# Expert feed-forward on TensorE: tokens transposed six parts ahead instead of four, and the low half of the tokens read last

## The chip, the cores and the metric

The kernel is one program on one NeuronCore of a Trainium2 chip. The metric is device time in microseconds; the times of repeated executions and one profiled execution are given. The engines are TensorE (PE in the profile, with its weight loads as PEld), VectorE (DVE), ScalarE (ACT), GpSimd (POOL) and SyncE (SP), which only issues transfers here.

## What is computed

A cross-attention layer and then a mixture-of-experts feed-forward, in float32. The change lies in the second. Cut to what matters:

```python
# 16 experts, each takes its 256 best tokens out of 4096; D = 256, F = 1024
_, idx = jax.lax.top_k(logits.T, 256)
xe = xn[idx]                                             # [16, 256, 256] gathered tokens
h = jnp.einsum('ecd,efd->ecf', xe, fc1_weight) + fc1_bias[:, None, :]
h = jax.nn.gelu(h, approximate=False)
y = jnp.einsum('ecf,edf->ecd', h, fc2_weight) + fc2_bias[:, None, :]
contrib = (y * gates[:, :, None]).reshape(-1, d)
output = jnp.zeros((n_tokens, d)).at[idx.reshape(-1)].add(contrib)
```

## The kernel before, in words

The attention part takes the first 790 us of the span and is not touched. A search for each expert's limit follows, and from 843 us on the experts run one after the other.

Precision is kept by splitting: a float32 operand is written as a high part (a rounded copy, made by ScalarE) and a low part (the rest, made by VectorE or GpSimd), and a product of two such operands is three fast products: high by high, low by high, high by low. `xe_hi` and `xe_lo` are the two parts of an expert's tokens, `w1_hi` and `w1_lo` those of its first weights. Some products take plain float32 operands; TensorE runs each of them as two instructions.

For one expert `e` the pieces of work are:

- `gather`: GpSimd issues two indirect transfers that bring the 256 token rows into `gathered`.
- `turn_tokens`: TensorE transposes them, four 128x128 blocks into one PSUM bank (line 1175). ScalarE scales the bank into `xe_hi` (two instructions), and then VectorE makes `xe_lo` from the bank and `xe_hi` (line 2107, two instructions). The signal `xe_hi_made` (semaphore tokens_high) tells of the first, `xe_emptied` (semaphore tokens_split) of the second.
- `hidden(e, f)`, f = 0 to 7: the first product of the expert for 128 of the 1024 hidden values, six matmuls of 256 columns into one of four banks. ScalarE applies the gelu (`h_full`), and for f = 0 to 3 of the experts from 2 on the result is split as well (`h_hi`, `h_lo`).
- `expert_out(e, c, f)`: one of the eight parts of the second product, for token half c. For f = 0 to 3 it is three fast matmuls (`in_parts`), for f = 4 to 7 one float32 matmul (two instructions). Half c = 0 takes f in the order 0 to 7, half c = 1 in the order 4, 5, 6, 7, 0, 1, 2, 3. Experts 0 and 1 use float32 for all parts.
- `gate`, `scale_out`, `scatter`: bias, gate value, and the transfer that adds the rows to the output.
- `split`, `split_out`: the weights of the next experts are split (ScalarE, then GpSimd or VectorE). `list_hot`, `list_count`, `list_join`, `list_spread`: which tokens belong to a later pair of experts.

One list, `schedule_experts()`, sets the order of all of it. Each engine's program walks the list and takes the kinds that concern it. Within an expert a counter `at` goes up after every `hidden` and every `expert_out`, 24 in all, and `between()` adds the other work at given counts. Waits are issued through `Waits.wait_ge`, which skips a wait for a value that the engine has already waited for, so that a wait in `hidden` for the tokens is issued once per expert, at f = 0. In the rows of instructions below `w_0` with `h_full` is a float32 part of the second product, `w_hi` and `w_lo` are split weights: with `xe_hi`, `xe_lo` those of the first product, with `h_hi`, `h_lo` those of the second.

Of the kernel before, what the change touches and what calls it, by code (L numbers as in the profile page):

```python
# [26 lines left out]
E, F = 16, 1024  # L27
# [7 lines left out]
FT = F // P  # L35
# [310 lines left out]
def group_of(e):  # L346

    return e if e < 2 else e // 2 + 1


def schedule_experts():
    plan = []

    def add(*piece):
        plan.append(piece)
# [54 lines left out]
    def second_list(at):  # L410

        if at == 5:
            add("list_count", 2)
            add("list_join", 2)
        elif at == 7:
            add("list_spread", 2)
            add("gather", 2)
            add("gather_gates", 1)
# [7 lines left out]
    for e in range(1, E):  # L426
        lists = group_of(e + 3) if e % 2 and e + 3 < E else None
        counts = group_of(e + 2) if e % 2 == 0 and e + 2 < E else None
        state = {"point": 0}
        hot_points = (8, 9) if e == 1 else (9, 17)  # L430

        def between():

            state["point"] += 1
            at = state["point"]
            if e == 1:
                second_list(at)
            if at == 10 and e == 1:
                for c in range(2):
                    add("scale_out", 0, c)  # L440
            if at == 2 and counts:
                add("list_count", counts)
            if at == 5 and counts:
                add("list_join", counts)
            if at == 7 and counts:
                add("list_spread", counts)
            if at == (11 if e == 1 else 4):
                for c in range(2):
                    add("scatter", e - 1, c)
            if at == 9 and 2 < e + 1 < E:  # L450
                add("split", e + 1, 1)
            if at == 13 and e + 2 < E:
                add("split", e + 2, 0)
            if at == (12 if e == 1 else 10) and e + 2 < E:
                add("gather", e + 2)
            if at in hot_points and lists:
                add("list_hot", lists, hot_points.index(at))
            if at == 3 * FT - 4 and e + 1 < E:
                add("turn_tokens", e + 1)
            if at == 3 * FT - 2 and e + 1 >= SPLIT_FROM and e + 1 < E:  # L460
                add("split_out", e + 1)

        for f in range(FT):
            add("hidden", e, f)
            between()
        for c in range(2):
            for f in OUT_ORDER[c]:
                add("expert_out", e, c, f)
                between()
            add("gate", e, c)  # L470
            if e == E - 1:
                add("scale_out", e, c)
                add("scatter", e, c)
        if e < E - 1:
            for c in range(2):
                add("scale_out", e, c)
# [8 lines left out]
def _build(nc, io, everything):  # L485
# [3 lines left out]
    def signal(name):  # L489
        return Signal(semaphore(name))  # L490

    def sb(name, shape, dt, where=None):
        return (where or everything).enter_context(nc.sbuf_tensor(name, shape, dt))
# [85 lines left out]
    w1_hi, w1_lo = ([sb(f"w1_{n}{i}", [P, 2, F], F32R) for i in range(2)] for n in ("hi", "lo"))  # L579
# [5 lines left out]
    xe_hi, xe_lo = ([sb(f"xe_{n}{i}", [P, 2, CAP], F32R) for i in range(2)] for n in ("hi", "lo"))  # L585
# [61 lines left out]
    def token_key(e, c):  # L647

        return (e, c if c is not None else 1) if e == 0 else (e,)
# [55 lines left out]
    xe_hi_made = signal("tokens_high")  # L705
# [129 lines left out]
    turned, xe_emptied = signal("tokens_turned"), signal("tokens_split")  # L835
# [77 lines left out]
    def tensor_program(pe):  # L913
        on = Waits(pe)

        def mm(out, lhsT, rhs, start, stop):
            return pe.matmul(out, lhsT, rhs, start=start, stop=stop, skip_group_check=True)  # L917
# [260 lines left out]

        def hidden(e, f):
            i = e % 2  # L1180
            on.wait_ge(*xe_emptied.at(*token_key(e, 1)))
            for n in range(2):
                on.wait_ge(*w_lo_made.at(e, n))
            n = e * FT + f
            if n >= 4:
                on.wait_ge(*h_made.at(*hidden_order[n - 4]))
            to, cols, n = hidden_bank[n % 4][:, 0:CAP], slice(f * P, (f + 1) * P), 0
            for half in range(2):
                for w, x in ((w1_hi, xe_hi), (w1_lo, xe_hi), (w1_hi, xe_lo)):
                    last = mm(to, w[i][:, half, cols], x[i][:, half, :], n == 0, n == 5)  # L1190
                    n += 1
            last.then_inc(hidden_filled.sem, 1)

        def expert_out(e, c, f):
# [18 lines left out]
            if f == last_f:  # L1213
                last.then_inc(y_filled.sem, 1)

        work = {"search": search, "limits": limits, "rank": rank, "list_count": list_count, "list_spread": list_spread,
                "turn_tokens": turn_tokens, "hidden": hidden, "expert_out": expert_out}
        for kind, *at in expert_plan:
            if kind in work:
# [1119 lines left out]
```

## Time and profile before

| | us |
|---|---|
| median of 3 executions | 1089.4 (1089.0 to 1089.87) |
| profiled execution, its own time | 1088.49 |
| profiled execution, span of the core | 1086.7 |
| TensorE matmuls busy | 981.4 (90% of the span) |
| VectorE busy | 788.4 (73%) |
| ScalarE busy | 675.7 (62%) |
| GpSimd busy | 767.8 (71%) |

The span is the stretch from the first to the last instruction that the profiler recorded; the execution's own time lies 1.79 us above it. Busy times are sums over instructions and say nothing yet on which engine sets the end in a given stage.

### The profile page before, as it was taken

The page shows a single profiled execution, that of the slowest core. Times are in us where ns is not written, and L with a number is a line of the kernel's source. Part 1 is how long each engine was busy: PE and PEld are TensorE (multiplying, and loading weights), DVE is VectorE, ACT ScalarE, POOL GpSimd, SP SyncE. Part 2 cuts the span into 40 slices and gives each one's busy share as a digit, 9 for nine tenths or more (in the row PEclk, how much of TensorE's full clock was granted, in tenths as well). Part 3 has the DMA queues.
Part 4 walks back from the last instruction along what each step waited for, and adds up shares of the span by engine and source line. Part 5 has one row for each costly group of instructions (what it writes and reads, how often), then busy time and mean ns, then how long its engine had stood idle before and what let it go on. Part 6 is the DMA issues. An engine that isn't in the chain of part 4 may idle for free. (4 is left out here: it accounts for less than half of the span.)

```text
span 1086.7 us, 17837 instructions
## 1 busy us (share of the span) xinstructions
PE 981.4 (90%) x6102; PEld 651.6 (60%) x6102; DVE 788.4 (73%) x1925; ACT 675.7 (62%) x1352; POOL 767.8 (71%) x872
## 2 busy tenths in 40 slices
PE   4999999999999999999998999999811999999995
PEld 3665456555655655655564565444411889999995
DVE  6989778867977886887797677767588756666642
ACT  6775775766777677576757665554354446666662
POOL 4037997798698699679967967899313377777772
PEclk9899999999999999999999999999955899999998
DMA  7020020002012001210110001000174366666651
GB/s 188 1 63 2 6 59 1 1 28 59 1 27 80 1 1 54 54 50 12 46 46 2 4 1 42 13 1 21 40 194 129 41 182 197 197 205 205 205 167 20
DMA packets 73611, 71.82 MB, mean 66 GB/s; under 512 B 38928, under 2 KB 67568, under 8 KB 69424
## 3 DMA queue, kind: packets, MB, share of 16 engines
q1 hardware_dynamic: 66464, 61.92, 18.5%
q0 software_dynamic: 6272, 8.69, 4.6%
q8 instruction: 49, 0.80, 0.3%
q14 instruction: 42, 0.34, 0.1%
q10 hardware_dynamic: 784, 0.07, 0.1%
HBM read 56.83 MB, written 13.83 MB: 65 GB/s over the span
## 5 line engine op out<-in xcount | busy, mean ns | idle before, releaser
L1504 POOL TENSOR_TENSOR prob_sum<-prob_sum,probs 128x256 f32<-128x256 f32 x628 | 467.2, 775 | 79.4 <-ACT probs L1227 71.0
L917 PE MATMUL bank<-probs,v_nat 128*64 128x512 f32 x768 | 190.0, 609 | 0.5 <-ACT probs L1227 0.5
L1819 DVE CUSTOM_DVE_ANT_0 masked_scores<-score_pair,mask_bias 128x512 bf16<-128x512 f32 x142 | 92.1, 686 | 49.1 <-PE score_pair L917 47.8
L1227 ACT ACTIVATE probs<-score_pair,mask_col 128x512 f32<-128x512 f32 x128 | 81.0, 686 | 66.9 <-PE score_pair L917 64.6
L1227 ACT ACTIVATE probs<-pair_bank,mask_col 128x512 f32<-128x512 f32 x128 | 81.3, 690 | 49.5 <-PE pair_bank L917 37.1
L917 PEld LDWEIGHTS bank<-probs,v_nat 128*64 128x64 f32 x768 | 46.0, 136 | 84.2 <-issue 77.6
L1819 DVE CUSTOM_DVE_ANT_0 masked_scores<-pair_bank,mask_bias 128x512 bf16<-128x512 f32 x114 | 73.9, 685 | 25.4 <-PE pair_bank L917 24.0
L1570 POOL DMA_INDIRECT out_x<-y_out,token_index x32 | 54.9, 1714 | 40.6 <-DVE y_out L2139 36.0
L1534 POOL TENSOR_TENSOR w_lo<-w_raw,w_hi 128x1024 fp32r<-128x1024 f32 x28 | 66.4, 2371 | 20.9 <-ACT w_hi L1227 20.5
L1504 POOL TENSOR_TENSOR prob_sum<-probs 128x256 f32<-128x256 f32 x64 | 44.9, 733 | 46.7 <-ACT probs L1227 40.0
L1812 DVE TENSOR_REDUCE maxima<-pair_bank 128x2 f32<-128x1024 f32 x42 | 51.1, 1217 | 25.2 <-PE pair_bank L917 24.9
L1227 ACT ACTIVATE h_full<-bank,b_cols 128x256 f32<-128x256 f32 x96 | 44.1, 468 | 35.8 <-PE bank L917 35.7
L1482 POOL TENSOR_TENSOR z_lo<-z_full,z_hi 128x512 fp32r<-128x512 f32 x32 | 40.9, 1280 | 33.9 <-ACT z_hi L1227 33.9
L917 PE MATMUL bank<-xe_hi,w_hi 128*128 128x256 f32 x192 | 57.7, 300 | 5.9 <-DVE xe_lo L2107 5.9
L1850 DVE RECIPROCAL bank<-bank 128x128 f32<-128x128 f32 x64 | 57.3, 934 | 3.4 <-PE bank L917 3.4
L917 PE MATMUL bank<-w_ctx_hi,z_hi 128*128 128x512 f32 x128 | 56.9, 445 | 0.8 <-POOL z_hi L1482 0.8
L917 PE MATMUL bank<-xe_hi,w_lo 128*128 128x256 f32 x192 | 54.5, 284 | 0.0
L917 PE MATMUL bank<-xe_lo,w_hi 128*128 128x256 f32 x192 | 54.5, 284 | 0.0
L1227 ACT ACTIVATE squares<-bank 128x256 f32<-128x256 f32 (+1 forms) x96 | 44.2, 460 | 15.8 <-PE bank L917 8.5
L1617 DVE TENSOR_REDUCE sq_sum<-squares 128x4 f32<-128x256 f32 (+1 forms) x96 | 46.0, 497 | 9.2 <-ACT squares L1227 9.1
L1227 ACT ACTIVATE probs<-pair_bank 128x512 f32<-128x512 f32 x58 | 31.4, 594 | 32.4 <-PE pair_bank L917 27.9
L1227 ACT ACTIVATE probs<-score_pair 128x512 f32<-128x512 f32 x70 | 38.0, 596 | 21.4 <-PE score_pair L917 19.1
(278 smaller groups left out, 2796.6 us busy)
## 6 DMA issues: line engine op xcount, KB each, us to landing
w_raw<-in_fc SPq DMA_DIRECT2D x16, 1024.0 KB, 4.9
w<-in_fc SPq DMA_DIRECT2D x16, 1024.0 KB, 5.8
c_in<-in_ctx SPq DMA_DIRECT2D x16, 384.0 KB, 4.1
x_in<-in_x SPq DMA_DIRECT2D x8, 512.0 KB, 5.0
out_x<-x_in SPq DMA_DIRECT2D x8, 512.0 KB, 3.9
rows_scratch<-xr_nat SPq DMA_DIRECT2D x8, 512.0 KB, 3.0
c_in<-in_ctx SPq DMA_DIRECT2D x16, 128.0 KB, 4.2
b_rows<-in_fc_bias SPq DMA_DIRECT2D x16, 128.0 KB, 5.6
```

The lines of the kernel that those rows point to most:

```text
L917: return pe.matmul(out, lhsT, rhs, start=start, stop=stop, skip_group_check=True)
L1227: return act.activation(out, a, f, bias=bias, scale=scale)
L1482: tt(to[place][rows, half, :], z_full[rows, half, :], as32(z_hi[place][rows, half, :]), ALU.subtract).then_inc(z_lo_made.sem, 1)
L1504: last = tt(total[:, half], first[:, half], p[:, half], ALU.add)
L1534: tt(w1_lo[i][:, n, :], w1_raw[i][:, n, :], as32(w1_hi[i][:, n, :]), ALU.subtract).then_inc(w_lo_made.sem, 1)
L1570: pool.indirect_dma_start(out_rows, bass.IndirectOffsetOnAxis(ap=tokens_of(e, c), axis=0), y_out[i][:, c, :], None, compute_op=ALU.add).th ...
L1617: dve.tensor_reduce(sq_sum[:, place:place + heads], squares[square_turn[use] % 2][:, 0:heads * DH].rearrange("p (h d) -> p h d", d=DH), AX ...
L1812: last = dve.tensor_reduce(maxima[:, :, j, g], place[:], AX, ALU.max)
L1819: last = dve.tensor_tensor_reduce(masked_scores[:, hh, :], place[:, hh, :], mask_bias[:, 512 * g:512 * (g + 1)], 1.0, MASKED, ALU.add, ALU ...
L1850: state["inverse", pair, quarter] = step.of(dve.reciprocal(sums, sums))
```

## The change

The transposes of the next expert's tokens are placed in the list when 18 of an expert's 24 pieces are issued, in place of 20, except in expert 1, where they stay at 20. And `hidden` waits at its head for the high part of the tokens alone, issues the four matmuls that read it, waits for the low part, and issues the two that read that. The number of instructions stays the same on every engine.

```diff
@@ schedule_experts()
                 add("gather", e + 2)
             if at in hot_points and lists:
                 add("list_hot", lists, hot_points.index(at))
-            if at == 3 * FT - 4 and e + 1 < E:
+            if at == (3 * FT - 4 if e == 1 else 3 * FT - 6) and e + 1 < E:
                 add("turn_tokens", e + 1)
@@ tensor_program: hidden(e, f)
             i = e % 2
-            on.wait_ge(*xe_emptied.at(*token_key(e, 1)))
+            on.wait_ge(*xe_hi_made.at(*token_key(e, 1)))
             for n in range(2):
                 on.wait_ge(*w_lo_made.at(e, n))
@@
             for half in range(2):
-                for w, x in ((w1_hi, xe_hi), (w1_lo, xe_hi), (w1_hi, xe_lo)):
-                    last = mm(to, w[i][:, half, cols], x[i][:, half, :], n == 0, n == 5)
+                for w in (w1_hi, w1_lo):
+                    mm(to, w[i][:, half, cols], xe_hi[i][:, half, :], n == 0, False)
                     n += 1
+            on.wait_ge(*xe_emptied.at(*token_key(e, 1)))
+            for half in range(2):
+                last = mm(to, w1_hi[i][:, half, cols], xe_lo[i][:, half, :], False, half == 1)
             last.then_inc(hidden_filled.sem, 1)
```

Two places of TensorE's row of instructions show what moved. The first is the second token half of expert 5, where the tokens of expert 6 are transposed (`ident,gathered`). Before:

```order
L917 MATMUL bank<-w_0,h_full 128x256 [waits hidden_made] x4
L917 MATMUL pair_bank<-w_0,h_full 128x256 [waits y_emptied]
L917 MATMUL pair_bank<-w_0,h_full 128x256 x3
L1175 MATMUL score_pair<-ident,gathered 128x128 [waits gathered2]
L1175 MATMUL score_pair<-ident,gathered 128x128 x3
L917 MATMUL pair_bank<-w_hi,h_hi 128x256
```

In the changed kernel, at the same place:

```order
L917 MATMUL bank<-w_0,h_full 128x256 [waits hidden_made] x4
L917 MATMUL pair_bank<-w_0,h_full 128x256 [waits y_emptied]
L917 MATMUL pair_bank<-w_0,h_full 128x256
L1175 MATMUL score_pair<-ident,gathered 128x128 [waits gathered2]
L1175 MATMUL score_pair<-ident,gathered 128x128 x3
L917 MATMUL pair_bank<-w_0,h_full 128x256 x2
L917 MATMUL pair_bank<-w_hi,h_hi 128x256
```

The four transposes went ahead of two float32 matmuls (four instructions on the chip, since each is run as two). No other row lies between.

The second place is the hand-over to the next expert, the end of expert 5's second product and expert 6's first `hidden`. Before:

```order
L917 MATMUL pair_bank<-w_hi,h_lo 128x256
L917 MATMUL bank<-xe_hi,w_hi 128x256 [waits expert_w_low,tokens_split]
L917 MATMUL bank<-xe_hi,w_lo 128x256
L917 MATMUL bank<-xe_lo,w_hi 128x256
L917 MATMUL bank<-xe_hi,w_hi 128x256
L917 MATMUL bank<-xe_hi,w_lo 128x256
L917 MATMUL bank<-xe_lo,w_hi 128x256
```

In the changed kernel:

```order
L917 MATMUL pair_bank<-w_hi,h_lo 128x256
L917 MATMUL bank<-xe_hi,w_hi 128x256 [waits expert_w_low,tokens_high]
L917 MATMUL bank<-xe_hi,w_lo 128x256
L917 MATMUL bank<-xe_hi,w_hi 128x256
L917 MATMUL bank<-xe_hi,w_lo 128x256
L917 MATMUL bank<-xe_lo,w_hi 128x256 [waits tokens_split]
L917 MATMUL bank<-xe_lo,w_hi 128x256
```

The two matmuls that read `xe_lo` went to the end of the group, and the wait for tokens_split went with them. On VectorE, ScalarE, GpSimd and SyncE no row moved.

## Rows read from the trace of the kernel before

**Rows 1.** Head of the page.

```profile
span 1086.7 us, 17837 instructions
```

**Rows 2.** Windows: two experts, the first products of expert 0, a stretch near 880.

```profile
core 0: us, PE busy (x) PEld busy (x) DVE busy (x) ACT busy (x) POOL busy (x), PEclk, DMA share, GB/s
925.07:953.09 28.02, 27.20 (x219) 25.48 (x219) 17.33 (x30) 17.41 (x34) 20.50 (x13) 1.00 0.65 197
...
847.35:851.30 3.95, 3.95 (x16) 3.38 (x17) 1.87 (x3) 1.55 (x3) 1.39 (x1) 0.50 0.26 71
...
878.60:882.00 3.40, 3.40 (x11) 2.80 (x10) 1.77 (x3) 1.78 (x3) 2.79 (x3) 0.50 0.54 56
```

**Rows 3.** Waits of the weight loads, 880 us to the end: total, times, longest.

```profile
PEld bank L917 <- DVE xe_lo L2107: 8.0, 13, 0.6
```

**Rows 4.** Timeline of TensorE, hand-over from expert 5 to 6: start, duration, instruction.

```profile
934.02 1.89 PE L917 MATMUL pair_bank<-w,h_full 128*128 128x256 f32 x8
935.75 0.60 PE L1175 MATMUL score_pair<-ident,gathered 128*128 128x128 f32 x4
936.11 0.36 PE L917 MATMUL pair_bank<-w_hi,h_hi 128*128 128x256 f32 x1
...
937.38 0.28 PE L917 MATMUL pair_bank<-w_lo,h_hi 128*128 128x256 f32 x1
937.50 0.28 PE L917 MATMUL pair_bank<-w_hi,h_lo 128*128 128x256 f32 x1
938.19 0.38 PE L917 MATMUL bank<-xe_hi,w_hi 128*128 128x256 f32 x1 [0.41 <-DVE xe_lo L2107]
938.41 0.28 PE L917 MATMUL bank<-xe_hi,w_lo 128*128 128x256 f32 x1
```

**Rows 5.** Timeline of GpSimd, VectorE and ScalarE over the same hand-over.

```profile
932.58 2.35 POOL L1534 TENSOR_TENSOR w_lo<-w_raw,w_hi 128x1024 fp32r<-128x1024 f32 x1
...
935.14 1.21 DVE L2068 TENSOR_TENSOR hot_ids<-hot_lo,tile_ids 128x1024 bf16<-128x1024 bf16 x1
...
936.39 0.84 ACT L1227 ACTIVATE xe_hi<-score_pair,nw_col 128x256 fp32r<-128x256 f32 x2 [2.96 <-PE score_pair L1175]
...
937.12 1.06 ACT L1227 ACTIVATE w_hi<-w 128x1024 fp32r<-128x1024 f32 x1
...
937.26 0.87 DVE L2107 SCALAR_TENSOR_TENSOR xe_lo<-score_pair,nw_col,xe_hi 128x256 fp32r<-128x256 f32 x2 [0.91 <-ACT xe_hi L1227]
```

**Rows 6.** A gather for expert 7, its landing times, and the transposes that read it.

```profile
936.42 0.98 POOL L1552 DMA_INDIRECT gathered<-rows_scratch,token_index  x1 [0.30 <-issue]
...
DMA to landing us min/median/max: 2.8/5.0/6.3
...
950.64 0.60 PE L1175 MATMUL score_pair<-ident,gathered 128*128 128x128 f32 x4
```

**Rows 7.** Timeline of all engines, start of expert 0.

```profile
846.02 0.63 ACT L1227 ACTIVATE xe_hi<-score_pair,nw_col 128x128 fp32r<-128x128 f32 x2 [1.49 <-PE score_pair L1175]
...
846.15 0.58 PE L917 MATMUL bank<-earlier,all_ones 128*128 128x448 bf16 x1
...
846.68 0.61 DVE L2107 SCALAR_TENSOR_TENSOR xe_lo<-score_pair,nw_col,xe_hi 128x128 fp32r<-128x128 f32 x2
...
847.35 0.58 PE L917 MATMUL bank<-xe_hi,w_hi 128*128 128x256 f32 x1 [0.62 <-DVE xe_lo L2107]
847.73 0.41 PE L917 MATMUL bank<-xe_hi,w_lo 128*128 128x256 f32 x1
```

**Rows 8.** Chain that ended last, 847 to 879 us: start, duration, what.

```profile
855.69 0.88 DVE xe_lo L2107 x2
...
873.12 5.16 DMA gathered<-rows_scratch,token_index
```

**Rows 9.** Timeline of TensorE, end of expert 1.

```profile
878.33 0.92 PE L1175 MATMUL score_pair<-ident,gathered 128*128 128x128 f32 x4 [2.22 <-DMA gathered<-rows_scratch,token_index]
879.04 3.35 PE L917 MATMUL pair_bank<-w,h_full 128*128 128x256 f32 x8
```

## The prediction, made before the changed kernel was run

> **What bounds the kernel now.** The page gives the span, 1086.7 us [rows 1], and TensorE as the busiest engine. Busy shares don't say which wait costs time, so I read the expert stage by windows next. Over two consecutive experts, 28.02 us, TensorE's matmuls are busy 27.20 us at the full granted clock of 1.00, GpSimd 20.50, ScalarE 17.41 and VectorE 17.33 [rows 2]. TensorE sets the pace there, and only what makes it stop can be won. The waits from 880 us on name one stop alone that recurs: 13 times the weight loads stood still until VectorE's `xe_lo` was there, 8.0 us in all [rows 3]. These are the 13 hand-overs from one expert to the next, from expert 2 to 3 up to 14 to 15.
>
> The timeline shows one of them [rows 4]. The last matmul of expert 5 starts at 937.50, and the first of expert 6 at 938.19. The cause is a chain that begins with the transposes at 935.75. ScalarE starts `xe_hi` at 936.39, VectorE starts `xe_lo` at 937.26 and needs 0.87 [rows 5], and TensorE starts at 938.19, 0.06 after the end of `xe_lo`. From the transposes to the first product is thus 2.44 us, while the second product behind the transposes gives TensorE only 1.87 us of work (935.75 to 937.62).
>
> **What one stop costs.** The matmul row shows 0.41 idle, but matmuls are pipelined and overlap, so I take starts. Undisturbed fast matmuls start 0.12 apart (937.38, 937.50). From 937.50 to the second matmul of the next expert, at 938.41, pass 0.91, where two steps of 0.12 would do: 0.67 is lost [rows 4]. Times 13 that is 8.7 us. Taken from the weight loads it would be 8.0 [rows 3], and from the matmuls' idle time 13 x 0.41 = 5.3; these are the low bounds. The Trainium skill, page "Perfetto Trace Analysis", section "Identifying the Most-Contended Engine", says that matmul busy time is a poor measure of how near TensorE is to its limit, since pipelined instructions look smaller than they are, and that weight-load busy time is better. By that the sum would be 8.0 and not 5.3. The trace agrees in direction; the starts give a little more than either.
>
> **First edit: transposes two parts ahead.** They now pass two float32 parts, four of the eight instructions that start between 934.02 and 935.75, so 4 x 0.216 = 0.87 us [rows 4]. The whole chain moves up by that, if its engines are free. ScalarE is: it had been idle 2.96 us when `xe_hi` came [rows 5]. VectorE in this expert has a list to build, `hot_ids` until 936.35; `xe_lo` would be released at 937.26 - 0.87 = 936.39, so it just fits; the even experts make no such list. `xe_lo` is then ready for TensorE at 938.19 - 0.87 = 937.32, and TensorE comes for it at 937.62 at the earliest. The stop is gone, with 0.30 to spare.
>
> The transposes cost TensorE the same wherever they stand. The four take 0.36 from first start to the next instruction [rows 4]. What the trace doesn't show at full clock is transposes followed by float32 matmuls. At half clock it does: the first float32 matmul comes 0.71 behind four transposes [rows 9], no more than twice 0.36. The bounds are 0 and, from the step that is 0.10 longer after the present stop (938.19 to 938.41 against 0.12), 0.10 for each of 13, 1.3 us together. I take 0, since the row with the same sequence shows none.
>
> **Second edit: low part last.** The first four matmuls now need `xe_hi` only, which VectorE started to use at 937.26, and the low part is wanted four steps of 0.12 later, 0.48 us. Alone this edit would leave 938.19 - (937.62 + 0.48) = 0.09 of the stop. With the first edit in place it adds nothing in these 13 hand-overs but slack: 0.30 becomes 0.78. The added wait stands in front of two matmuls with nothing but later matmuls of TensorE behind it; it is issued once per expert and is satisfied when it comes. I take nothing for it: the list has such waits at most of the `hidden` pieces already, and TensorE's 27.20 busy plus two stops of 0.41 are the whole 28.02 of two experts [rows 2, 4], so a satisfied wait leaves no idle time.
>
> The second edit acts alone in expert 0. There TensorE stands from the end of a list product until `xe_lo` is there at 847.35, while `xe_hi` is done at 846.65 [rows 7]. The list product's row ends at 846.73, with a tail that overlaps the next matmul, and 0.06 behind `xe_hi` is 846.71: TensorE can start the first product there, 0.64 earlier. Sixteen matmuls take 3.95 at this clock [rows 2], about 0.25 each, so the four high ones reach past 847.35 and no second stop follows. What of the 0.64 reaches the end? The chain that ended last goes on through expert 0's first products, expert 1's `xe_lo` at 855.69, VectorE's gate work and list, the gather that lands at 878.3, and the transposes at 878.33 [rows 8, 9]. All of it hangs on TensorE here, so it moves along. But TensorE works at half clock until 851.3 (0.50) [rows 2]: if the clock rises at the same moment whatever TensorE does, 0.64 us gained at half speed is worth 0.32 afterwards. Bounds 0.3 and 0.64; I take 0.45, the middle.
>
> In expert 1 the transposes stay where they are, and behind them lie eight float32 instructions, enough. Nothing changes.
>
> **What comes next to the bound.** With the stop gone two experts take 28.02 - 1.34 = 26.68 us. GpSimd's 20.50 fits. Its `w_lo` for the next expert was done at 934.93 for a product at 938.19 [rows 5], 3.3 us early, and remains 2.6 early. VectorE's later work gets easier: the split of the second weights starts when ScalarE's `w_hi` ends, 938.18 before, and both move up with the transposes. The gather for expert 7 was issued at 936.42 and takes 5.0, at most 6.3, so it is there by 942.7, against 950.64 - 0.87 = 949.77 for its transposes, 7 us of slack [rows 6].
>
> **The sum.** 8.7 + 0.45 = 9.15 us off the profiled execution's own 1088.49 gives 1079.3. That execution lay 0.9 below the median of the three runs, so for the median 1089.4 - 9.15 = 1080.2.
>
> **The rivals.**
>
> *As forecast*, the 13 stops vanish and nothing takes their place: 1080.2. Chance 0.74.
>
> *A new wait takes part of it.* VectorE is the candidate in the experts that build lists, five of the 13: `hot_ids` ends only 0.04 before `xe_lo` would be released. For it speaks that margin; against it the 0.78 of slack behind. It would need to be 0.78 late there. If half of all the stops came back, the gain would be 4.35 + 0.45 = 4.8: 1084.6. Chance 0.10.
>
> *The clock falls out otherwise.* After TensorE's wait of 2.22 us for the gather, the granted clock is 0.50 from 878.6 to 882.0 [rows 2], and the four transposes and eight matmuls take 0.71 and 3.35 against 0.36 and 1.89 at full clock: 1.8 lost [rows 4, 9]. The first product starts earlier now, and everything behind lies differently against the clock. If this stretch is spared, 1078.4; if it comes twice, 1082.0. The three runs of before lie within 0.9 us, which speaks for a steady clock. Chance 0.10. The Trainium skill, page "TensorE: Matmul & The Clock Gate", section "What's actually happening", says that the moment of the clock's change isn't tied to the kernel's start and varies from run to run. By that rule both outcomes should turn up among single runs of either kernel; so far no run here shows it.
>
> *It doesn't bind.* If another engine or a transfer set the pace of two experts at 28.02, the stops would only change their name: 1089.4. Against it, no other engine exceeds 20.50 and no other wait recurs. Chance 0.03.
>
> *Slower.* The transposes now ask for the gathered rows 0.87 earlier and hold everything behind them on TensorE, since they stand in its queue. Were the rows late, the stop would lie there, in the middle of the second product. It decides when a landing takes over 13.3 us (936.42 to 949.77) instead of 5.0, and costs net from 14.0 on, 0.67 being won back. With rows 1 us late at all 13 it is 13 x 0.33 - 0.45 = 3.8 slower: 1093.2. In the trace only expert 2's rows came late [rows 9], and there the place is unchanged. Chance 0.03.
>
> **How the numbers follow.** A measurement of this kernel can tell about 0.2%, 2.2 us. Faster by more: forecast, part and clock, 0.94. Within: 0.03. Slower: 0.03. The likeliest case alone reaches from 1079.2 (8.7, 0.64, and 0.9 for the spread of the runs) to 1082.4 (weight-load count 8.0, 0.3, and the full 1.3 for the changed sequence). The range takes in the clock case on both sides and a small part of the second rival: 1078.3 to 1083.0, some 85 in 100.
>
> **What would show it.** In the profile of the changed kernel: the waits of the weight loads for `xe_lo` in the expert stage go from 13 times to none; the last matmul of an expert and the first of the next start 0.12 apart, at every hand-over; two experts take 26.7 us; `xe_lo` ends 0.3 us before the old first product's place; expert 0's first product starts right behind `xe_hi`, at about 846.7. The prediction is wrong if a wait of similar size appears under another name (gathered, `h_lo`, `w_lo`), if transposes between float32 matmuls cost a step, or if the granted clock of the stage differs from 1.00.

## The result, and the profile after

| | before | the changed kernel |
|---|---|---|
| median, us | 1089.2 (1086.79 to 1090.39, 6 runs) | 1079.34 (1077.77 to 1080.65, 6 runs) |
| profiled execution, its own time | 1088.49 | 1077.77 |
| span of the core | 1086.7 | 1075.9 |

The ratio of changed to before is 0.9916, 95% interval 0.9906 to 0.9926. That is a gain of 0.84%; by the ratio it is 9.15 us, by the two medians 9.9. The changed kernel was timed once more beside its variants (the last experiments below) and came out at 0.9919, interval 0.9907 to 0.9932.

The spans differ by 10.8 us, and 1.73 of that has nothing to do with the change: in this execution the part ahead of the experts ended earlier. The cut is the list product in front of expert 0's first product (`bank<-earlier,all_ones`), which starts at 846.15 before [rows 7] and at 844.42 after. What lies behind it differs by 9.07 us, against the 9.15 of the prediction's sum. That the two agree to 0.1 is partly luck: a second profiled execution of the changed kernel (`after_again` below) differs by 9.7 behind the same cut, since its clock fell out otherwise.

First the head of the changed kernel's page, then its windows over the two experts that correspond to [rows 2], from the first product of expert 5 to that of expert 7, and over a stretch near 880 us.

```profile
span 1075.9 us, 17837 instructions
```

```profile
core 0: us, PE busy (x) PEld busy (x) DVE busy (x) ACT busy (x) POOL busy (x), PEclk, DMA share, GB/s
921.02:947.75 26.73, 26.73 (x221) 25.39 (x220) 19.69 (x31) 17.39 (x34) 20.50 (x13) 1.00 0.68 209
877.30:880.70 3.40, 3.40 (x13) 2.87 (x12) 2.83 (x6) 1.41 (x3) 3.06 (x2) 0.50 0.68 77
```

Two experts take 26.73 us in place of 28.02, and the matmuls are busy in all of them. VectorE went from 17.33 to 19.69 us, although it executes the same instructions. The stretch at a granted clock of 0.50 (1.2 GHz of the two levels 1.2 and 2.4) is there as before, 3.4 us long.

The waits of the changed kernel's weight loads from 880 us on. The row of [rows 3] is gone, and what is left are five short waits of another kind:

```profile
PEld score_pair L917 <- DVE list_parts L2085: 0.8, 5, 0.2
```

The timeline of TensorE in the changed kernel, at the hand-over from expert 5 to 6, to be laid beside [rows 4]:

```profile
930.74 0.60 PE L1175 MATMUL score_pair<-ident,gathered 128*128 128x128 f32 x4
931.18 1.03 PE L917 MATMUL pair_bank<-w,h_full 128*128 128x256 f32 x4
...
933.35 0.28 PE L917 MATMUL pair_bank<-w_hi,h_lo 128*128 128x256 f32 x1
933.47 0.28 PE L917 MATMUL bank<-xe_hi,w_hi 128*128 128x256 f32 x1
...
933.95 0.40 PE L917 MATMUL bank<-xe_lo,w_hi 128*128 128x256 f32 x2
934.19 0.28 PE L917 MATMUL bank<-xe_hi,w_hi 128*128 128x256 f32 x1
```

The last product of expert 5 and the first of expert 6 start 0.12 apart, and it is 0.12 at the other twelve hand-overs too. From the transposes to the first product 2.73 us pass now, all of them work; before it was 2.44 with a stop in them.

GpSimd, VectorE and ScalarE over the same hand-over, for [rows 5]:

```profile
928.54 2.93 POOL L1537 TENSOR_TENSOR w_lo<-w_raw,w_hi 128x1024 fp32r<-128x1024 f32 x1
...
933.95 2.39 POOL L1537 TENSOR_TENSOR w_lo<-w_raw,w_hi 128x1024 fp32r<-128x1024 f32 x1
```

```profile
930.48 1.29 DVE L2070 TENSOR_SCALAR hot_ids<-hot_lo,token_in_tile 128x1024 bf16<-128x1024 bf16 x1
931.69 1.21 DVE L2071 TENSOR_TENSOR hot_ids<-hot_lo,tile_ids 128x1024 bf16<-128x1024 bf16 x1
932.82 0.86 DVE L2110 SCALAR_TENSOR_TENSOR xe_lo<-score_pair,nw_col,xe_hi 128x256 fp32r<-128x256 f32 x2
933.61 3.82 DVE L2118 TENSOR_TENSOR w_lo<-w,w_hi 128x1024 fp32r<-128x1024 f32 x1
```

```profile
931.38 0.84 ACT L1230 ACTIVATE xe_hi<-score_pair,nw_col 128x256 fp32r<-128x256 f32 x2 [2.10 <-PE score_pair L1175]
```

`xe_hi` is done at 932.22, but `xe_lo` doesn't start before 932.82, since VectorE still works at the list. It ends at 933.68, which is 0.21 us behind the start of the first product (933.47) and 0.27 ahead of the first product that reads it (933.95). In this expert it is the second edit that keeps TensorE from stopping.

Last, the start of expert 0 and the transposes of expert 2 in the changed kernel, for [rows 7] and [rows 9]:

```profile
844.42 0.58 PE L917 MATMUL bank<-earlier,all_ones 128*128 128x448 bf16 x1
...
844.97 0.29 PEld L917 LDWEIGHTS bank<-xe_hi,w_hi 128*128 128x128 f32 x1 [0.77 <-ACT xe_hi L1230]
844.97 0.58 PE L917 MATMUL bank<-xe_hi,w_hi 128*128 128x256 f32 x1
```

```profile
876.23 0.66 PE L1175 MATMUL score_pair<-ident,gathered 128*128 128x128 f32 x4 [1.96 <-DMA gathered<-rows_scratch,token_index]
876.73 3.09 PE L917 MATMUL pair_bank<-w,h_full 128*128 128x256 f32 x8
879.25 0.78 PE L917 MATMUL bank<-xe_hi,w_hi 128*128 128x256 f32 x1
```

The first product of expert 0 starts 0.55 behind the start of the list product, where it was 1.20. The wait for the gathered rows of expert 2 is 1.96 in place of 2.22.

To see what each stretch gave, the table sets out intervals between starts on TensorE's timeline for every kernel of this study, in us. A is the list product, 0, 2 and 3 are the first products of those experts, T the transposes of expert 2, and "end" is the last product of expert 15. The variants are told below.

| kernel | A to 0 | A to T | T to 2 | 2 to 3 | 3 to end | span |
|---|---|---|---|---|---|---|
| before | 1.20 | 32.18 | 3.72 | 14.98 | 178.40 | 1086.7 |
| the changed kernel | 0.55 | 31.81 | 3.02 | 15.06 | 170.37 | 1075.9 |
| after_again | 0.55 | 31.67 | 2.03 | 15.05 | 170.85 | 1075.9 |
| turn_only | 1.20 | 32.26 | 3.69 | 14.43 | 172.07 | 1079.5 |
| low_last_only | 0.55 | 32.14 | 3.48 | 14.67 | 172.82 | 1081.0 |
| expert0_only | 0.55 | 31.95 | 3.42 | 15.29 | 178.30 | 1086.4 |
| list_behind | 1.19 | 32.14 | 3.71 | 14.43 | 190.07 | 1099.0 |
| turn_16 | 1.19 | 32.31 | 3.71 | 14.40 | 188.81 | 1096.0 |
| half_pool | 0.55 | 30.03 | 2.03 | 14.41 | 170.23 | 1075.9 |
| e1_22 | 0.55 | 31.97 | 1.59 | 15.50 | 170.81 | 1076.1 |
| e1_24 | 0.55 | 31.87 | 1.59 | 15.16 | 170.35 | 1074.9 |
| gates_clear | 0.55 | 29.12 | 2.03 | 20.78 | 170.35 | 1080.0 |
| best | 0.55 | 29.75 | 1.53 | 20.03 | 170.38 | 1080.1 |
| early_list | 0.55 | 29.18 | 2.03 | 17.14 | 170.71 | 1076.2 |

Of the 9.07 us, 8.03 lie in the last stretch, with 12 of the 13 hand-overs: 0.67 each. The thirteenth, from expert 2 to 3, is hidden in the table: the half-clock stretch began 1.07 us behind the transposes of expert 2 instead of 0.27 (877.3 and 876.23, against 878.6 and 878.33), so that less of it lay ahead of expert 2's first product (3.72 became 3.02) and more behind (14.98 became 15.06). The two columns together, T to 3, went from 18.70 to 18.08: 0.62. From A to T 0.37 came from expert 0, and 0.05 lies behind the last product.

### The profile page after: what moved, and what is told of

It is laid out like the page before. It is cut to its first block and busy times, and to the rows that moved or that the text cites. A ratio compares the mean times of both kernels' runs of the same rounds, so it can differ in the third digit from the quotient of the medians.

```text
span 1075.9 us, 17837 instructions
## 1 busy us (share of the span) xinstructions
PE 975.3 (91%) x6102; PEld 649.4 (60%) x6102; DVE 801.7 (75%) x1925; ACT 675.0 (63%) x1352; POOL 768.3 (71%) x872
## 5 line engine op out<-in xcount | busy, mean ns | idle before, releaser
L1537 POOL TENSOR_TENSOR w_lo<-w_raw,w_hi 128x1024 fp32r<-128x1024 f32 x28 | 70.3, 2511 | 13.3 <-ACT w_hi L1230 13.1
L917 PE MATMUL bank<-xe_hi,w_hi 128*128 128x256 f32 x192 | 53.0, 297 | 0.0
L917 PE MATMUL bank<-xe_hi,w_lo 128*128 128x256 f32 x192 | 51.1, 287 | 0.0
L917 PE MATMUL bank<-w_ctx_lo,z_hi 128*128 128x512 f32 x128 | 51.0, 398 | 0.0
```

The lines of the kernel that those rows point to most:

```text
L1537: tt(w1_lo[i][:, n, :], w1_raw[i][:, n, :], as32(w1_hi[i][:, n, :]), ALU.subtract).then_inc(w_lo_made.sem, 1)
```

## The experiments

### Each edit alone

`turn_only` is the kernel before with the first edit, `low_last_only` with the second as its diff above shows it, and `expert0_only` with the second in expert 0 alone.

```diff
@@ turn_only: schedule_experts()
-            if at == 3 * FT - 4 and e + 1 < E:
+            if at == (3 * FT - 4 if e == 1 else 3 * FT - 6) and e + 1 < E:
@@ expert0_only: hidden(e, f)
-            on.wait_ge(*xe_emptied.at(*token_key(e, 1)))
+            on.wait_ge(*(xe_emptied if e else xe_hi_made).at(*token_key(e, 1)))
...
+            if e == 0:
+                passes = [(half, *p) for part in (high, low) for half in range(2) for p in part]
```

> The transposes stand six parts ahead, the first product reads its inputs in the old order with the one wait at its head. Theory of the prediction: the low part is there 0.30 us before it is wanted at all 13 hand-overs, so every stop vanishes, 8.7 us gained, ratio about 0.992, and the second edit is worth only the 0.45 us of expert 0. Rival, from the trace of the changed kernel: in experts 3, 5, 7, 9 and 11 VectorE is held up by its list work and the low part ends 0.22 us behind the first product's place; then five stops of about 0.38 us stay and the gain is 8.7 - 1.9 = 6.8 us, ratio about 0.994.

> The transposes stay four parts ahead, the first product reads the low part last. Theory of the prediction: 0.09 us of each stop stays at the low products, up to 0.2 with the slower restart behind a stop; gain 13 x 0.48 to 13 x 0.58 plus 0.45 in expert 0, 6.7 to 8.0 us, ratio 0.9927 to 0.9939. Rival that a wait in the middle of a group of products costs more than it hides: stops of 0.3 us and more stay, gain under 5 us.

> Only expert 0 reads the low part last; all else is as before. Theory: its first product starts 0.65 us earlier, and 0.3 to 0.64 us of that is left where expert 2's tokens are transposed, so that the stretch from the list product before expert 0 to those transposes is 0.3 to 0.64 us shorter than the 32.18 us of before. Rival: the gather's landing or VectorE's list sets that place whatever TensorE does, and the stretch stays at 32.2. In whole time both are within what a measurement can tell. The 13 stops of 0.67 us stay.

| | median, us | ratio to before, 95% interval |
|---|---|---|
| turn_only | 1081.8 | 0.9947 (0.9934 to 0.996) |
| low_last_only | 1081.87 | 0.9941 (0.9928 to 0.9954) |
| expert0_only | 1087.68 | 0.9991 (0.9979 to 1.0003) |

**Transposes ahead alone** leave the stop in five of the thirteen hand-overs. Waits of its weight loads from 880 us on:

```profile
PEld bank L917 <- DVE xe_lo L2107: 1.6, 5, 0.3
```

TensorE and VectorE at one of the five, expert 5 to 6:

```profile
935.65 0.28 PE L917 MATMUL pair_bank<-w_hi,h_lo 128*128 128x256 f32 x1
936.05 0.39 PE L917 MATMUL bank<-xe_hi,w_hi 128*128 128x256 f32 x1
936.28 0.28 PE L917 MATMUL bank<-xe_hi,w_lo 128*128 128x256 f32 x1
```

```profile
935.13 0.86 DVE L2107 SCALAR_TENSOR_TENSOR xe_lo<-score_pair,nw_col,xe_hi 128x256 fp32r<-128x256 f32 x2
```

The step is 0.40 where 0.12 is undisturbed. The other four, at 908.6, 962.7, 989.8 and 1016.8, look the same (0.38 or 0.40); all five follow an expert that builds a list (3, 5, 7, 9, 11). So the rival of the expectation is what came. The prediction's step that the first edit removes all thirteen stops by itself is wrong in these five. The last column of the table prices them: 172.07 against 170.37 with both edits, 1.70 us, 0.34 each.

**Low part last alone** takes 178.40 down to 172.82, 0.465 for each of twelve hand-overs, and leaves 0.205 of 0.67. The prediction left 0.09. Its gain, 6.4 us by the ratio, is just under the 6.7 that was the least expected. The timeline of TensorE in this kernel, same hand-over, shows the difference:

```profile
936.53 0.28 PE L917 MATMUL pair_bank<-w_hi,h_lo 128*128 128x256 f32 x1
936.65 0.28 PE L917 MATMUL bank<-xe_hi,w_hi 128*128 128x256 f32 x1
...
937.01 0.28 PE L917 MATMUL bank<-xe_hi,w_lo 128*128 128x256 f32 x1
937.22 0.50 PE L917 MATMUL bank<-xe_lo,w_hi 128*128 128x256 f32 x2
937.56 0.28 PE L917 MATMUL bank<-xe_hi,w_hi 128*128 128x256 f32 x1
```

The low products start 0.21 behind the fourth high one, 0.09 more than a step, as reckoned. But the two of them then take 0.34 to the next product, where two take 0.24 undisturbed (933.95 to 934.19 in the changed kernel). Behind the stop of [rows 4] the next step was 0.10 longer than the usual 0.12, and so it is here, where the stop is 0.09; 0.09 + 0.10 is the 0.2 that stayed. What makes that step longer no run shows.

**Expert 0 alone** moves its first product up by 0.65, and the transposes of expert 2 by 0.23 (32.18 to 31.95). Its total can't be told from that of the kernel before.

### Why VectorE is late in the list-building experts

In `list_behind` (the first edit, and the second list piece at 19 in place of 17) VectorE makes `xe_lo` before that piece; in `turn_16` the transposes stand at 16, without the second edit. Both clear `xe_lo`'s way.

```diff
@@ list_behind, beside the first edit
-        hot_points = (8, 9) if e == 1 else (9, 17)
+        hot_points = (8, 9) if e == 1 else (9, 19)
@@ turn_16
-            if at == 3 * FT - 4 and e + 1 < E:
+            if at == (3 * FT - 4 if e == 1 else 3 * FT - 8) and e + 1 < E:
```

> As turn_only, with the second piece of VectorE's list work for a later pair of experts placed behind the split of the tokens instead of ahead of it. If the list work ahead of it is what makes the low part late in five experts, all 13 stops vanish without the second edit: gain 8.7 us, ratio about 0.992, 1.9 us faster than turn_only. If VectorE is late for another reason (GpSimd's work on the weights at the same time), the five stops stay and the time is that of turn_only.

> First product in the old order, transposes eight parts ahead in place of six (expert 1 as before), so that VectorE's split of the tokens stands ahead of the second piece of its list work. Theory: what made the low part late in five experts with six parts ahead is that VectorE was still at that list piece; here the low part is ready about 0.9 us before it is wanted at all 13 hand-overs, no stop is left without the second edit, and the list piece is done before the long split of the second weights: 8.7 us gained, ratio about 0.992. Rival: the list piece is pushed back as it was with the list behind the split, the count of the list waits 2.8 us in five experts, and the time is above the kernel before.

Both are slower than the kernel before: 1099.79 us, ratio 1.0101 (1.0088 to 1.0114), and 1097.4, ratio 1.0091 (1.0077 to 1.0104). No stop for `xe_lo` is left at any hand-over, in either. That was expected, but a gain of 8.7 us with it; only the rival of `turn_16` forecast the loss. In the stops' place stands this, in `list_behind`, five times; TensorE, VectorE and GpSimd behind the hand-over to expert 6, and the window that follows:

```profile
941.98 0.28 PE L917 MATMUL bank<-xe_lo,w_hi 128*128 128x256 f32 x1
944.75 0.96 PE L917 MATMUL score_pair<-hot_ids,hot_hi 128*32 128x64 bf16 x15 [2.49 <-DVE hot_ids L2068]
```

```profile
940.64 3.97 DVE L2068 TENSOR_TENSOR hot_ids<-hot_lo,tile_ids 128x1024 bf16<-128x1024 bf16 x1
```

```profile
941.15 2.37 POOL L1534 TENSOR_TENSOR w_lo<-w_raw,w_hi 128x1024 fp32r<-128x1024 f32 x1
```

```profile
944.50:947.90 3.40, 3.15 (x38) 3.09 (x39) 2.77 (x7) 0.00 (x0) 1.28 (x1) 0.50 0.62 246
```

`hot_ids` takes 1.21 us elsewhere and 3.97 here, where GpSimd's subtraction for `w_lo` lies inside it. TensorE stops for 2.77 from start to start, and the granted clock is then 0.50 for 3.4 us. Against the changed kernel the last stretch of the table is 19.7 us longer (190.07 against 170.37), 3.94 for each of the five: 2.65 is the stop (2.77 less a step of 0.12), and the 1.3 that is left goes to the half clock. In `turn_16` it is the other `hot_ids` instruction, at 937.92: 3.38 us long, 0.49 elsewhere, with `w_lo` on GpSimd from 938.61 to 941.01. The stops are 2.43 there and the five together 18.4 us.

`half_pool` is the test of the cause: the changed kernel, with GpSimd's subtraction done for one half of the weights' columns only, for the experts from 2 on (the other half is left out, so the result isn't the reference's).

```diff
-                tt(w1_lo[i][:, n, :], w1_raw[i][:, n, :], as32(w1_hi[i][:, n, :]),
+                half = slice(0, F // 2)
+                tt(w1_lo[i][:, n, half], w1_raw[i][:, n, half], as32(w1_hi[i][:, n, half]),
```

> The changed kernel, with GpSimd's subtraction for the first weights cut to half of its columns from expert 2 on: half of w1_lo is then that of an earlier expert, which leaves part of the work out. If GpSimd and VectorE take turns at these subtractions, VectorE's split of the second weights (3.57 and 3.82 us beside GpSimd's 2.4) falls by about half of GpSimd's time, to 2.4 to 2.7, and the low part of the tokens in experts 3, 5, 7, 9 and 11 ends before the first product starts instead of 0.22 us behind. If VectorE is slow for its own reasons, both stay. The time stays within 1 us of the changed kernel, as TensorE has no stop there.

Groups of VectorE's instructions by line and form (count, busy us in all, mean ns of one, idle before), in the kernel before:

```profile
L2115 DVE TENSOR_TENSOR w_lo<-w,w_hi 128x1024 fp32r<-128x1024 f32 x14 | 34.8, 2484 | 1.0
L2067 DVE TENSOR_SCALAR hot_ids<-hot_lo,token_in_tile 128x1024 bf16<-128x1024 bf16 x7 | 4.0, 573 | 0.1
```

The same two in the changed kernel:

```profile
L2118 DVE TENSOR_TENSOR w_lo<-w,w_hi 128x1024 fp32r<-128x1024 f32 x14 | 47.0, 3355 | 0.6
L2070 DVE TENSOR_SCALAR hot_ids<-hot_lo,token_in_tile 128x1024 bf16<-128x1024 bf16 x7 | 7.4, 1063 | 0.1
```

And with half of GpSimd's subtraction left out:

```profile
L2119 DVE TENSOR_TENSOR w_lo<-w,w_hi 128x1024 fp32r<-128x1024 f32 x14 | 23.2, 1658 | 1.0
L2071 DVE TENSOR_SCALAR hot_ids<-hot_lo,token_in_tile 128x1024 bf16<-128x1024 bf16 x7 | 3.9, 562 | 0.1
```

Nothing of VectorE's own was changed, and both groups fall by half. VectorE at the hand-over to expert 6, in this kernel:

```profile
931.06 1.21 DVE L2072 TENSOR_TENSOR hot_ids<-hot_lo,tile_ids 128x1024 bf16<-128x1024 bf16 x1
932.29 0.87 DVE L2111 SCALAR_TENSOR_TENSOR xe_lo<-score_pair,nw_col,xe_hi 128x256 fp32r<-128x256 f32 x2
```

`xe_lo` ends 0.35 ahead of the first product (933.51), as at the others. So it is GpSimd's subtraction that makes VectorE late, and not the list by itself, which is all still there. The two take turns.

The last stretch of the table, 170.23 against 170.37, says that this cost TensorE nothing in the changed kernel from expert 3 on. The one time, 1077.76 us, doesn't say so for the whole: in this execution the list product A started at 847.89, 3.47 later than in that of the changed kernel, and what lies behind it is 3.5 us shorter. Of that 1.78 lie between A and T, where GpSimd's subtraction for expert 2 stands beside VectorE's gate work (taken up below), and 1.64 between T and 3, where this execution has no half clock. The Trainium skill, page "GPSIMD Engine Reference", section "Specifications", says that GpSimd shares its SBUF interfaces with VectorE and contends with instructions of VectorE that read two SBUF inputs or run in a two-port mode. The trace agrees: `w_lo` and the second `hot_ids` read two tiles in SBUF. The first `hot_ids` reads one and grew too; in which mode it ran the trace doesn't show.

### The wait for expert 2's rows, and the half clock behind it

The changed kernel with expert 1's transposes (20 there) at 22 and at 24:

```diff
-            if at == (3 * FT - 4 if e == 1 else 3 * FT - 6) and e + 1 < E:
+            if at == (3 * FT - 2 if e == 1 else 3 * FT - 6) and e + 1 < E:
```

> The changed kernel, with the transposes of expert 2's tokens at 22 of 24 pieces in place of 20. They wait for a gather that lands at a fixed time, and two more float32 parts are done in that wait instead of behind it. The first product of expert 2 then waits for the high part, 1.5 us behind the transposes, in place of 3.0 us: 1 to 2 us faster than the changed kernel. Rival: the clock falls in the longer row of small stops and eats it, no change.

> The same with the transposes behind all 24 pieces of expert 1, so that all four float32 parts fill the wait. The first product of expert 2 starts 1.5 us behind the transposes: 1.5 to 2.2 us faster than the changed kernel, if the second weights of expert 2 have landed when ScalarE comes to split them, which now stands ahead of the tokens. Rival: they have not, ScalarE waits for them with the tokens behind it, and the time is that of the changed kernel or more.

1078.2 us, ratio 0.9911 (0.9896 to 0.9927), and 1079.06, ratio 0.9921 (0.9908 to 0.9935): neither can be told from the changed kernel, so the 1 to 2 us expected didn't come. The wait for the gathered rows falls from 1.96 to 1.4 and 0.5, no half clock follows in their profiled executions, and T to 2 shrinks to 1.59, for there is also less of expert 1's second product behind the transposes. But at 24 TensorE stands 0.9 for `xe_hi` behind the transposes, and 0.2 for `xe_lo`. A to T stays at 31.87 to 31.97 in both: the rows land when they land. And from T to 3 there are 17.09 and 16.75 us, against 18.08 and 17.08 in the two profiled executions of the changed kernel: most of what the shorter T to 2 gave is no more than the spared half clock, or comes back as a wait for `list_parts`.

### The changed kernel again, and three variants beside it

`gates_clear` is the changed kernel with GpSimd's `w_lo` for expert 2 (part of its first weights; the expectation calls them the second) held until expert 2's ids are made, and the gathering of the gates behind that of expert 2's rows. `best` has expert 1's transposes at 22 besides. `early_list` has the list of expert 2 counted at 3 and its rows gathered at 5, in place of 5 and 7, and expert 1's transposes at 20.

```diff
@@ gates_clear: schedule_experts()
-            add("gather_gates", 0)
...
+            add("gather_gates", 0)
@@ gates_clear: GpSimd's w_lo
+            if e == 2:
+                on.wait_ge(*ids_made.at(2, 0))
@@ early_list, besides
-        if at == 5:
+        if at == 3:
...
-        elif at == 7:
+        elif at == 5:
```

> The changed kernel itself once more, on the chip that runs the three variants of it beside it, so that they can be compared with it there. Expected: its ratio to the kernel before as already measured, 0.9916 within 0.001, so about 1079 us, and the same marks in its trace: 3.0 us from the transposes of expert 2 to its first product, and one stretch at half clock about 33 us behind the list product that precedes expert 0.

> The changed kernel, but GpSimd begins its subtraction for expert 2's second weights (the tile w_lo) only once the ids of expert 2's tokens are made, and the gathering of the gates is issued behind the gathering of expert 2's rows. Theory: VectorE's gate work for expert 2 is long because GpSimd's subtraction lies beside it (gate_sum 1.39 us and all_probs 2.38 us, against 0.32 and 1.30 us in the kernel whose subtraction is halved). With it clear of that stretch they should take about 0.3 us and 0.6 to 1.3 us, the transposes of expert 2 should start sooner or the wait for its gathered rows be shorter by 1 to 2 us, and the kernel should be 0.7 to 1.8 us faster than the changed one. Rival: TensorE's own order decides when the list of expert 2 is counted, and the time of the gathering does the rest; then gate_sum gets shorter, and the first product of expert 2 and the total stay within 0.3 us of the changed kernel.

> The previous kernel with the four transposes of expert 1 two steps later (at 22 in place of 20), so that TensorE has that much of expert 0's work before it. Theory: the wait for the first rows and the half clock that follows it go; with the gate work shorter as well, the wait for expert 2's rows is at most 0.5 us, and the kernel is 2 to 3 us faster than the changed one. Rival: expert 1's own products then wait for their turned rows and take back what expert 2 gains; then it is within 0.5 us of the changed kernel.

> The kernel with GpSimd's subtraction held back, and besides the list of expert 2 counted and joined at step 3 of the hidden products in place of 5, and its rows gathered at 5 in place of 7; expert 1's transposes stay at 20. Theory: the wait for expert 2's rows comes from the list being made late on TensorE; two steps are 3.3 us, so the rows land before TensorE wants them, no stop and no half clock follow, and the kernel is 3 to 4.5 us faster than the changed one. Rival: the list waits at step 3 for VectorE's work, which is not done sooner, so that a stop stands there in place of the one before the transposes; then the gain is under 1 us or a loss.

| | median, us | ratio to before, 95% interval |
|---|---|---|
| after_again | 1078.88 | 0.9919 (0.9907 to 0.9932) |
| gates_clear | 1081.88 | 0.994 (0.9925 to 0.9954) |
| best | 1080.76 | 0.9932 (0.9919 to 0.9944) |
| early_list | 1077.03 | 0.9904 (0.9888 to 0.992) |

**The changed kernel again** has the same span to a tenth, 1075.9, and a clock that fell out otherwise. Its transposes of expert 2 and a window of the stretch that was at half clock before:

```profile
876.75 0.66 PE L1175 MATMUL score_pair<-ident,gathered 128*128 128x128 f32 x4 [1.86 <-DMA gathered<-rows_scratch,token_index]
877.25 1.89 PE L917 MATMUL pair_bank<-w,h_full 128*128 128x256 f32 x8
```

```profile
877.00:881.00 4.00, 4.00 (x42) 3.66 (x41) 2.61 (x5) 2.87 (x6) 3.39 (x3) 1.00 0.62 54
```

TensorE stopped for about as long (1.86 against 1.96 us), and this time the clock stayed at 1.00. The same kernel shows both, so the half clock here is a matter of the single execution. T to 2 is 0.99 shorter for it; 2 to 3 isn't, since a stop of 0.56 for `list_parts` stands there. Without that stop T to 3 would be 1.56 shorter than with the half clock, and in `half_pool`, which has neither, it is 1.64 shorter: about 1.6 us is the price of the stretch, where the prediction's clock rival reckoned 1.8.

This execution shows something else that the first doesn't. Among the waits of its weight loads from 880 us on is

```profile
PEld bank L917 <- DVE xe_lo L2110: 0.3, 1, 0.3
```

That is at the hand-over from expert 3 to 4, where `xe_lo` ended 0.24 behind the place of the low products and they started 0.30 late; expert 4 takes 0.50 longer, most of it for this, which is the whole difference between 170.85 and 170.37 in the table. The slack that the second edit gives is used up there.

**GpSimd held back** did on VectorE what was expected. In the changed kernel its gate work for expert 2 reads:

```profile
856.82 1.39 DVE L2055 SCALAR_TENSOR_TENSOR gate_sum<-gate_sum 128x32 f32<-128x32 f32 x1
```

In `gates_clear`:

```profile
858.70 0.19 DVE L2057 SCALAR_TENSOR_TENSOR gate_sum<-gate_sum 128x32 f32<-128x32 f32 x1
```

`all_probs` went from 2.38 to 0.69 us, and A to T fell by 2.55 us against `after_again`. And then 5.73 were lost between experts 2 and 3, in a way that none of my expectations named. VectorE's timeline, and TensorE's waits from 880 us on:

```profile
877.87 0.62 DVE L2144 TENSOR_SCALAR y_out<-y_out,gate_rows 128x256 f32<-128x256 f32 x2 [3.48 <-DMA gate_rows<-gates_scratch,token_index]
...
884.03 0.62 DVE L2144 TENSOR_SCALAR y_out<-y_out,gate_rows 128x256 f32<-128x256 f32 x2 [2.97 <-DMA gate_rows<-gates_scratch,token_index]
884.57 4.27 DVE L2126 TENSOR_TENSOR h_lo<-h_full,h_hi 128x256 fp32r<-128x256 f32 x4
888.76 0.20 DVE L2087 TENSOR_TENSOR list_parts<-score_pair,own_block 32x64 f32<-32x64 f32 x1
```

```profile
PE score_pair L917 <- DVE list_parts L2087: 3.3, 1, 3.3
```

The gate values, gathered later now, hold VectorE twice; `h_lo` and `list_parts` queue behind it, the four `h_lo` again beside GpSimd's subtraction (885.52, 2.35 us), and TensorE waits 3.3 us. The clock is at half from 889.2 to 892.7 after it. With the two edits in one kernel, which of them costs how much isn't separated; the row names the gates. `best` has the same stop at 2.8 us.

**The early list** is the only one of these three whose median lies below that of `after_again`, by 1.85 us, but the intervals of the ratios overlap, so a gain isn't shown. The 3 to 4.5 us expected didn't come. Its A to T is 2.49 shorter than in `after_again`, and a stop of 2.4 for `list_parts` in 2 to 3 takes most of it back.

## Why the prediction held, step by step

**The price of a stop** was right: 0.67 from starts, and 8.03 us over twelve hand-overs in the profile after. The two lower bounds, 8.0 from the weight loads and 5.3 from the idle time of the matmuls, were too low for the thirteen (8.7).

**The first edit alone removes all thirteen, with 0.30 to spare** was wrong. It holds for eight. The step that failed is "VectorE ... just fits": `xe_lo` was to be released when `xe_hi` ends, and was late by 0.60 (932.22 to 932.82). The forecast held `hot_ids` at its place behind the start of expert 5, and that much was right. What it left out is that `hot_ids` can take longer. Before, the first `hot_ids` starts 9.55 us behind the first product of expert 5 (925.07) and takes 0.60:

```profile
934.62 0.60 DVE L2067 TENSOR_SCALAR hot_ids<-hot_lo,token_in_tile 128x1024 bf16<-128x1024 bf16 x1
```

In the changed kernel it starts 9.46 behind (930.48, 921.02) and takes 1.29, beside GpSimd's `w_lo`. That one starts 7.5 behind the expert's start in both kernels, but takes 2.93 in place of 2.35. So the second `hot_ids` ends 11.88 behind the start in place of 11.28, and with it goes `xe_lo`. In `half_pool` the same list ends at 11.22, and `xe_lo` starts with the end of `xe_hi`. So nearly all of the 0.60 is GpSimd's doing, and the margin of 0.04 was too thin for any of it. Why GpSimd's instruction itself takes 0.6 longer stays open; in expert 13, which builds no list, it went from 2.35 to 2.86 as well, so `hot_ids` isn't the reason.

**The second edit adds nothing there but slack** was wrong with it, and the two errors cancel. The slack behind was given as 0.78 and was 0.27 in the list-building experts. This is the second rival's mechanism: VectorE used up 0.51 of the 0.78 that it would have needed for a stop, and in `after_again` it used up all of it once. Without the second edit it cost 1.7 us. That the second edit was there, for expert 0 and as slack that nothing was expected to need, is luck as far as the forecast goes.

**VectorE's later work gets easier** was wrong. `w_lo` on VectorE went from 34.8 to 47.0 us in all. TensorE didn't notice. GpSimd's `w_lo` was ready 2.0 ahead of the first product (931.47, 933.47), where 2.6 was forecast.

**Transposes between float32 matmuls cost 0** was right: 0.44 from the first transpose to the float32 matmul behind (930.74 to 931.18), and from the start of the token half's second product (929.88) to its last (933.35) 3.47 us, where it was 3.48 before (934.02 to 937.50). The hand-overs' full 0.67 leaves no room for the bound of 0.10.

**The second edit alone leaves 0.09** was half right; it leaves 0.2, with the 0.10 of the longer step behind the stop.

**Expert 0** gave 0.65 at its start, as reckoned (0.64), and 0.37 of it reached the transposes of expert 2 in the profile after, 0.23 in `expert0_only`, 0.04 in `low_last_only`. Kernels without the edit lie between 32.14 and 32.31 from A to T, so a single one is good to some 0.1; 0.3 is about what the edit is worth, my lower bound, and what a clock that rises at the same moment would leave. The rise of the clock fits it: it came 3.7 to 4.1 us behind expert 0's first product in the four profiled executions without the edit there, and 4.1 to 5.0 behind it in the ten with it, on average 0.8 later. It didn't move along with the product.

**The clock rival** was right as a mechanism and didn't decide: one profiled execution of the changed kernel had the stretch and one hadn't, at a price of 1.6 us, of which 1.0 was left between T and 3. What spoke against it, three runs within 0.9 us, was too few: six lie within 3.6 (1086.79 to 1090.39). The granted clock differs between the runs of one kernel as well, 0.962 on average over the span in the changed kernel's fastest and 0.958 in its slowest. The Trainium skill, page "TensorE: Matmul & The Clock Gate", section "What's actually happening", says that the moment of the change varies from run to run of a kernel, and these two executions agree.

In sum, from the columns of the table: 8.03 + 0.62 + 0.37 and 0.05 behind the last product make 9.07 us, where 8.7 + 0.45 = 9.15 was predicted.

## What to carry to other kernels

When a chain is moved ahead and a margin of some hundredths is left to the work of another engine, reckon that work with the length it has beside everything that can come to lie next to it, and not with the length it had. Two edits with the same aim aren't redundant because one covers the other on paper: here each alone gave 6 us, and the second was the cover for an error in the first. Before a piece of VectorE's list is moved next to work of GpSimd that reads SBUF, look at both timelines: moved by two pieces, it made the kernel 1% slower than it had been with all its stops.

## What was not expected of the hardware

- VectorE and GpSimd took turns at the cost of VectorE: 1.21 us became 3.82 and 3.97, 0.49 became 3.38, and an instruction on 32 columns (`gate_sum`) went from 0.19 to 1.39, while GpSimd's own 2.35 grew to 2.94 at most, and that not only where VectorE's list lay beside it. VectorE's instruction had in several cases started first (940.64 against 941.15).
- A stop of TensorE of 2.4 to 2.8 us was followed by 3.4 us at half clock all ten times in `list_behind` and `turn_16`; a wait of 2.4 in `early_list` was not, and one of 1.9 to 2.0 in the changed kernel once in two executions.
- The first step of TensorE behind a stop was 0.10 us longer, behind one of 0.09 as well as at the hand-overs of the kernel before.
